# Thirteen of seventeen passes written out in the instruction streams instead of looped over on the engines

## The reference, cut to what matters

```python
mod = (silu(c) @ wmod).reshape(16, 6, 1, 128)          # shifts, scales and gates of each sequence
h = layernorm(x) * (1 + ca) + sa
x = x + ga * attn(h)      # attn: layernorm, then h + mamba(forward) + flip(mamba(flip(.)))
h = layernorm(x) * (1 + cb) + sb
x = x + gb * ffn(h)       # ffn: one shared expert plus the 2 best of 8 experts, each silu(h@w1)*(h@w2)@w3
# mamba: u = silu(conv4(Win u)), dt = softplus(...), and for each of 16 states n:
#   h_n[t] = exp(dt[t] * A_n) * h_n[t-1] + dt[t] * u[t] * B_n[t];   y[t] += h_n[t] * C_n[t]
```

## Time and profile before

| what | value |
|---|---|
| median of 3 runs | 2608.17 us (2607.06 to 2610.25) |
| profiled execution | 2608.1 us |
| its span | 2606.3 us |
| first scan of pass 1, of pass 2, of pass 15 | 214.72, 367.34, 2377.11 us after the start of the span |
| DVE, POOL, PE, ACT busy | 88%, 75%, 81%, 58% of the span |

### The profile page before, as it was taken

The page is one execution under the profiler, slowest core; times in us unless marked ns, Lnnn a source line. Parts: engine busy times, 40 slices in busy tenths (PEclk is TensorE's granted clock), DMA queues, the critical chain, the costliest instruction groups (busy, mean ns, idle before and its releaser), DMA issues. The chain is left out here.

```text
span 2606.3 us, 37957 instructions
## 1 busy us (share of the span) xinstructions
PE 2115.5 (81%) x9893; PEld 1352.7 (52%) x9893; DVE 2288.7 (88%) x3603; ACT 1510.3 (58%) x2468; POOL 1957.9 (75%) x1437
## 2 busy tenths in 40 slices
PE   3677887878788797888879788797978879798868
PEld 1244554545555455555546555454555545555554
DVE  1699998989899898998989899899989989899973
ACT  2546656655565665656666555665556566565633
POOL 1577878778787877878777787877878787787854
PEclk8777998989899898998989899898989989899989
DMA  2334233333323333332333323233332333333310
GB/s 82 129 130 138 102 131 106 110 127 113 130 98 128 108 114 122 113 125 103 114 124 115 135 97 130 106 109 127 113 130 97 128 108 114 122 113 124 114 67 5
DMA packets 120494, 293.33 MB, mean 113 GB/s; under 512 B 18516, under 2 KB 53172, under 8 KB 120388
## 3 DMA queue, kind: packets, MB, share of 16 engines
q1 hardware_dynamic: 120388, 292.30, 32.8%
HBM read 285.91 MB, written 6.34 MB: 112 GB/s over the span
## 5 line engine op out<-in xcount | busy, mean ns | idle before, releaser
L426 POOL TENSOR_TENSOR bt<-v,bb 128x1024 f32<-128x1024 f32 x512 | 1207.1, 2361 | 176.5 <-DVE psA L787 173.7
L787 DVE TENSOR_TENSOR_SCAN psA<-psA,bt 128x512 f32<-128x512 f32 x1024 | 1199.4, 1218 | 114.4 <-POOL bt L426 91.6
L600 ACT ACTIVATE psA<-dt,aneg 128x512 f32<-128x512 f32 x1024 | 688.1, 688 | 821.0 <-DVE g L797 816.3
L987 PEld LDWEIGHTS psY<-ident,g 128*128 128x128 f32 x4096 | 519.4, 152 | 474.7 <-DVE g L797 262.3
L987 PE MATMUL psY<-ident,g 128*128 128x128 f32 x4096 | 608.6, 295 | 160.9 <-DVE g L797 160.7
L797 DVE TENSOR_TENSOR g<-psA,cb 128x512 f32<-128x512 f32 x1024 | 676.0, 680 | 0.0
L526 POOL TENSOR_TENSOR act<-pf,gf 128x512 f32<-128x512 f32 x288 | 366.2, 1272 | 252.1 <-DVE pf L882 220.9
L1068 PE MATMUL F<-h2T,w 128*128 128x512 f32 x576 | 334.2, 664 | 92.9 <-DVE pf L882 92.9
L1112 PE MATMUL F<-w,act 128*128 128x128 f32 x2304 | 318.6, 283 | 43.7 <-POOL act L526 41.7
L1112 PEld LDWEIGHTS F<-w,act 128*128 128x128 f32 x2304 | 291.4, 198 | 60.9 <-issue 53.9
L1071 PE MATMUL F<-h2T,w 128*128 128x512 f32 x576 | 308.9, 619 | 0.0
(11 more groups left out here) (133 smaller groups left out, 1724.6 us busy)
## 6 DMA issues: line engine op xcount, KB each, us to landing
bb<-bc_rows SPq DMA_DIRECT2D x256, 512.0 KB, 3.6
cb<-bc_rows SPq DMA_DIRECT2D x256, 512.0 KB, 3.6
x<-in_L_attn_x SPq DMA_DIRECT2D x16, 256.0 KB, 3.8
xR<-in_L_attn_x SPq DMA_DIRECT2D x16, 256.0 KB, 3.6
out_x<-osb SPq DMA_DIRECT2D x16, 256.0 KB, 3.9
w<-in_L_ffn_ew SPq DMA_DIRECT2D x2, 1024.0 KB
modA<-mod_table SPq DMA_DIRECT2D x16, 128.0 KB, 3.9
bc_rows<-xd SPq DMA_DIRECT2D x32, 64.0 KB, 3.0
```

The source lines that it names most:

```text
L426: g.tensor_tensor(bt[:, n % 2, :, :], v[d][:, :, :], bb[:, n // 2 % 2, n % 2, :].unsqueeze(1).broadcast_to([P, NH, T]), ALU.mult).then_inc ...
L600: s.activation(psA[:, half * T:half * T + T], dt_[d][:, half, :], ACT.Exp, scale=aneg[d][:, half, n:n + 1]).then_inc(a_s, 1)
L787: w.tensor_tensor_scan(ah, ah, bt[:, n % 2, half, :][:, order], 0.0, ALU.mult, ALU.add)\
L987: last = m.matmul(psY[:, half * T + i * P:half * T + i * P + P], g_[:, n % 2, half, i * P:i * P + P], ident[:, :], is_transpose=True, star ...
```

## The change

The loop on the engines is replaced by a Python loop. So the 13 bodies of passes 2 to 14 stand one behind the other in each of the five instruction streams, with `b` a number in each of them. The work, its order on each engine, the tiles, the transfers and the semaphores are the same, with the same targets.

```diff
             body(0, True, False, False)
             body(1, True, True, False)
-            with eng.Fori(2, NB - 1) as b:
+            for b in range(2, NB - 1):
                 body(b, True, True, False)
             body(NB - 1, True, True, True)
             body(NB, False, True, True)
```

## The result

The written-out kernel takes 2582.51 us (median of 6 runs, 2581.97 to 2583.46) against 2608.43 us of before beside it: 0.9901 of the time, with a 95% interval of 0.9888 to 0.9914. The forecast was 2583.

The account below looks back on a forecast made before the run. VectorE, busy 88% of the span, was the engine that hardly rests. Pieces summed to 24.3 us, whole passes to 25.7; 2608.1 - 25.7 + 0.5 = 2583 us (2582.9), with an 8 in 10 range of 2576 to 2597.

Parts of the forecast that it names:

- The comparison inside the kernel: Pass 1, already written out, takes 152.62 us; 13 such passes against the loop's 2009.77 us forecast 25.7 us gained.
- The back edge: Where the loop turns, VectorE gets no instruction for 2.9 us after its branch; 12 x 1.35 = 16.2 us removed.
- Slot 1: Slot of a pass where VectorE waits for TensorE's turned tiles in 8 turns; 8 x 0.49 = 3.9 us gained.
- Register work: Working out wait targets in the loop, unhidden where the engine itself is last; 4.3 us and 3.0 us gained in two slots.
- slot 6: Slot where VectorE waits for GpSimd's `bt`, delayed by GpSimd's register work; 0.33 x 13 = 4.3 us gained.
- Slots 0, 3, 4 and 8: Scans waiting for exponentials start later in written code, with a separate wait instruction; 0.06 x 4 x 13 = 3.1 us lost.
- Rival A: TensorE still falls to the lower clock in slots VectorE waits for; slot 1 hit in all passes, 2589 us; chance 0.11.
- Rival B: Straight code makes TensorE wait at each of 5 instruction packets a pass; 88 us more, 2670 us; chance 0.07.
- 78 more packets: Instruction packets the changed kernel fetches beyond before, about 13 x 6; their price already in pass 1's 152.62 us.
- Rivals C and D: C: the pass boundary's gap is not the branch, 2602.5 us, chance 0.05. D: nothing changes, 2608 us, chance 0.04.
- slot 31: Slot at the pass boundary, 5.81 us where the loop turns; forecast to take 4.46 us in each pass.

## Why the prediction was right

- **The comparison inside the kernel.** The sum was made from whole passes, 13 x 152.62 us for the stretch, and it came out at 13 passes of 152.62 to 152.82. The last addition and the store of an earlier sequence, which pass 1 lacks, cost nothing, as argued.
- **The back edge.** 1.35 us at each of 12 turns was forecast and 1.33 measured. Its cause was inferred from the rows of the branch; the hinted branch shows it, and the two runs with VectorE alone in or out of the loop show that no other engine has a part in it.
- **Slot 1.** All eight slow slots went, and none came back in any of the 13 passes. The one that the forecast left in (0.5 us) was not there. The hinted run and the one with VectorE alone written out take them away too, though TensorE still loops in both, so they are the back edge passed on to TensorE. One detail of the prediction was narrower than it said: only in four of the eight passes (4, 7, 10 and 13) were the eight matmuls of slot 0 at the lower clock. In the other four the clock fell just after them (1.25 us for the eight in pass 3, then 0.76 as the mean clock from 524.5 to 527.5 us).
- **Register work.** The sizes were right. The account of slot 6 was not: it gave all to GpSimd, and about 0.10 of 0.34 us are VectorE's own. That hurt no number here, as both engines were written out.
- **Slots 0, 3, 4 and 8.** The loss came as forecast, and its cause, the separate instruction for the late wait, is shown by the turned waits.
- **The total.** The forecast was 2582.9 us and 2582.5 were measured. The terms were off by some 0.3 us each, in both directions, so part of this closeness is luck: the errors cancelled, and the runs of the one kernel differ by 1.5 us.
- **Rival A** (the lower clock stays or moves): it lengthened none of the 13 passes. The lower clock did not go away, as its mean over them is 0.92 in both kernels; it lies where VectorE does not wait for TensorE. **Rival B** (straight code starves an engine): among the 13 passes one slot of VectorE was longer by 0.17 us (slot 10 of pass 2), and in pass 15 one by 0.35 (slot 3). Where 78 more packets were forecast, 63 came, 58 of them on q8, the queue that the prediction took for TensorE's. The prediction said that this queue moved nothing in the loop's passes; that holds for passes 3 to 14, but pass 2 had 5 packets. The instruction queues of the kernel after, over its whole span, where before had 20 and 86 packets:

```profile
q8 instruction: 78, 1.28, 0.2%
q14 instruction: 91, 0.75, 0.1%
```

  The other queue, q14, moved only 5 packets more, because VectorE's loop fetched its body anew in each turn. Over the whole span q14 had 27 packets with the hint, 56 with VectorE alone written out, 86 in before, 91 with all written out and 121 with VectorE alone in the loop. So VectorE's loop costs 59 of them (86 - 27) and its straight code 29 (56 - 27), while writing out the other engines adds 35 (91 - 56, and 121 - 86). The section of the Trainium skill on fetching (Runtime: NRT & Kernel Launch, Instruction fetch mechanics) calls the cost of going on to the next block mostly hidden. The trace agrees: 63 packets more, and on VectorE two longer slots, of 0.17 and 0.35 us.
- **Rivals C and D** fall: the trace of after has no branch of a loop, and slot 31 takes 4.47 us.

## What to carry to other kernels

Where some turns of a loop are already written out in the same kernel, their length against a turn's is the whole forecast, and the starts of one repeated instruction give it slot by slot. For each engine the time from its branch to the head of its body tells whether that head has to be fetched anew; if so, and if that engine sets the pace, a prefetch hint on it alone gives back most (here 18.5 of 25.9 us) without longer code, and writing out that one engine 21.6. In straight code, name first the wait that comes last, so that it hangs on the instruction itself, and check on the trace which slot's start it moves: turned where the other wait came last, it cost 0.07 us.

## What the runs showed of the hardware

- A body is late at its head depending on its length and its place: 229 instructions on GpSimd and 321 on ScalarE were there after 0.2 to 0.3 us, the same 321 at two other places after 3 us, 453 on GpSimd after 3.0 to 3.3, and VectorE's 454 after 2.7 to 3.1 at both places where they started. TensorE held about 1350 and lost about 2700. The Trainium skill (Runtime: NRT & Kernel Launch, Instruction fetch mechanics) gives 512 instructions for most engines and 2048 for TensorE. TensorE's rows agree. For the others the runs show less than that figure: the head of 454 was lost, with the body put at the start of a block.
- With the hint, VectorE's 454 instructions came in time, and the queue that serves it had fewer packets, not more: 27 in all against 86 in before, and none in passes 3 to 14. So with the hint the body was not fetched anew at all, which was not expected; why is open. The queue's row of the hinted kernel, over its whole span:

```profile
q14 instruction: 27, 0.22, 0.0%
```

- With ScalarE's head at place 100 the same queue had 148 packets, so it serves ScalarE as well, and the time was still within 2 us of before.
